# A decoder layer on one core: unit maxima turned as three bfloat16 parts, mask loads in two halves, penalty rows loaded earlier

## The chip, the cores and the metric

The kernel runs on one core of one Trainium2 chip. The metric is the device time of one execution in microseconds, a median over several runs. A profiled execution gives the trace; its own time is set beside its span, because every duration below comes from that one execution.

## What is computed

One post-norm decoder layer over x of 1024 tokens by 128 features, batch 1:

```
x = layernorm(x + self_attention(x))          # 16 heads of 8, one shared K and V head, no mask
x = layernorm(x + cross_attention(x, ctx))    # 16 heads of 8, ctx has 6404 keys
x = layernorm(x + ffn(x))                     # 8 experts, top-1, weighted by the router's maximum
scores = where(mask == 0, -1e9, Q @ K.T / sqrt(8)); softmax; @ V     # mask: int32, 1024 x 6404
```

The mask is 1024 rows of 6404 int32. In these inputs all its rows are alike, but the kernel reads all of it to find out: it counts in each column how many rows are live. The outputs are float32 and the scores need nearly float32 exactness, so queries and keys go to TensorE as a high and a low part.

## The kernel before, in words

**Units and steps.** A unit is two heads. There are 16 self units and 16 cross units (eight pairs of heads, twice, for the two halves of the tokens). The work of a unit is a row pass and a column pass. The row pass (`self_row`, L1518; cross: `row_products`, L1732) makes scores with tokens on partitions in a bank `RT`, and VectorE reduces each bank to maxima (L935; cross L952 and L953). The column pass (`self_col`, L1530; cross `col_product`, L1739) makes the same scores with keys on partitions in a bank `ST`, ScalarE takes exponentials (L1302), and TensorE multiplies them with the values into `O` (`add_values`, L1503). A self unit has 8 steps, a cross unit 10. The program is one list of steps `s`; step `s` does the column pass of step s, the row pass of step s + 16 and the values of step s - 1. So the row pass runs two self units ahead.

**The maxima.** The column pass needs the maximum subtracted. It enters as extra rows of the stacked operand: each head of a unit has 64 partitions of `Qs` (`STACK`), 32 of them hold the products of high and low parts (from partitions 1 and 67), and partitions 0, 33, 66 and 99 (`MAXROWS`) hold minus the maximum as a high and a low part for each of the two heads, against ones in K. Partitions 34 and 65 of K hold a penalty for masked keys (`PENROWS`).

The chain of one unit's maximum: VectorE folds the maxima (`finx`, L929); GpSimd splits them (`split_max`: a cast to float32r, L564, and a subtraction, L566); TensorE turns them against the identity (`turn_max`, L1481) into 16 partitions of `O`; ScalarE copies them to `mxr` (`max_copy`, L1238); SP loads them to the four rows of `Qs` (`max_rows`, issued at L315); TensorE waits for that load at the unit's first column (`have_max`). In the self units the turn stands 5 steps before that column (step 8g - 5), in the cross units 3 steps (`TURN`).

**The mask.** GpSimd issues 16 mask loads (`load_mask`, L541), each 128 rows by 3328 int32, into two buffers. Load m is issued when pass m - 2 is over and, from the fourth on, when the load of a named unit's max rows has landed (`max_in`). After each lands, GpSimd takes min(mask, 1) as bytes (L611) and adds them to a running sum (L617). The splits of the maxima of units 0 to 10 stand at fixed places between these passes (`MAX_AHEAD`, `MAX_BETWEEN`), all in GpSimd's one order; that of unit 11 follows the last pass, and behind it stands the first layernorm's work (L551 to L555), which TensorE needs at step 86.

**The queues.** GpSimd's loads go through one queue (q0, software), SP's through another (q1, hardware). Both use the core's 16 DMA engines.

**The penalty rows and the chunk.** At h = 13 of its list SP stores five pieces of the penalty to a DRAM row `pd`. At h = 14, after the max rows of unit 14, `more_keys` waits for the last chunk's keys and issues their four stores (L396). Behind these SP waits for the `pd` stores and loads `pd` to rows 34 and 65 of `Kr` and `Kc`. TensorE waits for those two loads (`pen_in`) before the first cross row, at step 112. GpSimd loads the chunk's keys only when the four stores have landed (`kd_more`).

Of the kernel before, what the change touches and what calls it, by code (L numbers as in the profile page):

```python
# [16 lines left out]
P = 128  # L17
# [21 lines left out]
MAXROWS = slice(0, 100, 33)  # L39
PENROWS = (34, 65)  # L40
# [5 lines left out]
LEAD = 16  # L46
SLOTS = 5
# [88 lines left out]
def decoder_layer(nc, t, out):  # L136
    ctx = ExitStack()
    with ctx:
# [51 lines left out]
        mxh = sb("mxh", [P, 2, 2, 4], F32R)  # L190
        mxr = sb("mxr", [16, 2, P])
# [39 lines left out]
        def experts_room(first):  # L231
# [31 lines left out]
            "rt_ready rt_free st_ready st_free pv mx mx_part mx_split mx_turned mx_copied max_in0 max_in1 "  # L263
# [49 lines left out]
        def _(sp):  # L313
# [24 lines left out]
            def max_rows(G):  # L338

                sp.wait_ge(S("mx_copied"), G + 1)  # L340
                load(Qs[MAXROWS, G % UNITS, :].bitcast(F32).rearrange("o (t f) -> o t f", f=P), mxr[:, G % 2, :],
                     f"max_in{G % 2}")
# [32 lines left out]
            def gather_x_queries(ph, parts=range(4)):  # L375

                if 0 not in parts:
                    for k in parts:
                        load(*q_part("x", k // 2, k % 2, 8 * ph, 8 * ph + 8), "xq_in")
                    return  # L380
                sp.wait_ge(S("pv"), 64 * (ph + 1))
                sp.wait_ge(S("xq_out"), 32 * (ph + 1))
                if ph:
                    sp.wait_ge(S("xq_in"), 80 * ph)
                load(Qs[MAXROWS, 8 * ph:8 * ph + 8, :].bitcast(F32).rearrange("o h q -> o (h q)"), zerof[:, :], "xq_in")
                for k in parts:
                    load(*q_part("x", k // 2, k % 2, 8 * ph, 8 * ph + 8), "xq_in")
# [22 lines left out]
            for h in range(UNITS):  # L410
# [88 lines left out]
        def _(pool):  # L499
# [22 lines left out]
            g_.memset(Qs[:, DIRECT:8, :].bitcast(F32), 0.0).then_inc(S("q_clean"), 1)  # L522

# [8 lines left out]
            def load_mask(m):  # L532
                q, w = m // 2, m % 2
                if m >= 2:
                    h = (m - 2) * 3 // 4
                    pool.wait_ge(S("mask_used"), m - 1)
                    if h:
                        pool.wait_ge(S(f"max_in{h % 2}"), 16 * (h // 2 + 1))
# [64 lines left out]
            for m in range(2 * QT):  # L603
# [4 lines left out]
                pool.wait_ge(S(f"mask_in{m % 2}"), 16 * (m // 2 + 1))  # L608
# [237 lines left out]
        def _(dve):  # L846
# [29 lines left out]
            for f in range(2):  # L876
# [4 lines left out]
                mark(v.tensor_tensor(rowc[:, f, 2:3], ident[:, 66 * f:66 * f + 1], ident[:, 66 * f + 33:66 * f + 34],  # L881
                                     ALU.add))
# [333 lines left out]
        def _(act):  # L1216
# [16 lines left out]
            def max_copy(G, bank=None):  # L1233
                act.wait_ge(S("mx_turned"), G + 1)
                if G >= 2:
                    act.wait_ge(S(f"max_in{G % 2}"), 16 * (G // 2))
                turned = O[0:16, 256:256 + P] if bank is None else ST[bank][0:16, 0:P]
                nc.scalar.copy(mxr[:, G % 2, :], turned).then_inc(S("mx_copied"), 1)  # L1238
# [178 lines left out]
        def _(pe):  # L1417
# [59 lines left out]
            def turn_max(G, bank=None):  # L1477
                pe.wait_ge(S("mx_split"), G + 1)
                rows = mxh[:, :, :, :].bitcast(F32).rearrange("p f k t -> p (f k t)")
                if bank is None:  # L1480
                    mm = mmul(O[0:16, 256:256 + P], rows, ident[:, :], start=False, stop=False, skip_group_check=True)  # L1481
                else:
                    mm = nc.tensor.transpose(ST[bank][0:16, 0:P], rows, ident[:, :])
                mm.then_inc(S("mx_turned"), 1)

            def have_max(G):
                pe.wait_ge(S(f"max_in{G % 2}"), 16 * (G // 2 + 1))
# [259 lines left out]
            def cross(gen):  # L1747
# [9 lines left out]
                def row(r, f):  # L1757
                    U, u = (r - SELF) // RU, (r - SELF) % RU
                    if f:
                        if u == 0 and U % 8 == 0:  # L1760
                            pe.wait_ge(S("xq_in"), 80 * (U // 8 + 1))
                            pe.wait_ge(S("pen_in"), 32)
# [193 lines left out]
```

## Time and profile before

| | us |
|---|---|
| median of 3 runs | 466.97 (466.77 to 467.68) |
| profiled execution, its own time | 469.97 |
| its span, first to last instruction | 467.7 |
| TensorE busy | 440.9 (94%) |
| VectorE busy | 396.7 (85%) |
| ScalarE busy | 358.4 (77%) |
| GpSimd busy | 245.1 (52%) |
| mean granted TensorE clock | 0.974 |

The page of the profile divides the span into 40 slices with each engine's busy share, the clock and the DMA rate. Behind it stand views of one line, one stretch or one tile, the chain of waits that ended last, and a timeline. TensorE's records are matmuls (PE) and weight loads (PEld). A float32 matmul is written as two records. An idle time in square brackets stands before the instruction and names who released it.

### The profile page before, as it was taken

To read this page: it belongs to the slowest core of one execution; us is meant where nothing else is said; L and a number is where in the kernel's file an instruction comes from. 1 tells how busy PE (TensorE), PEld (TensorE's weight loads), DVE (VectorE), ACT (ScalarE), POOL (GpSimd) and SP (SyncE) were. 2 spreads that over 40 slices of the span, in tenths; PEclk is the share of its full clock that TensorE was granted. 3 is DMA by queue.
4 is the path that set the end of the run, shared out by engine and by line. 5 is a ranking of instruction groups with operands and counts; after the bars stand their busy time and mean duration, and the time that the engine had idled before them with its cause. 6 is when DMAs were issued, how large, how long until landed. Compare 5 with 4: busy or idle time off the path is not lost.

```text
span 467.7 us, 10803 instructions
## 1 busy us (share of the span) xinstructions
PE 440.9 (94%) x3885; PEld 176.7 (38%) x3887; DVE 396.7 (85%) x522; ACT 358.4 (77%) x704; POOL 245.1 (52%) x381
## 2 busy tenths in 40 slices
PE   8999999999899999799999999999999999999983
PEld 2433333333334443233343334333443443333441
DVE  4989999999699689689998999999999999941455
ACT  6328889688677877588968988889868788878723
POOL 4726879976799604122447644444447254320453
PEclk9889999999899999989999999999999999999978
DMA  5849968679680073211232346322212122110000
GB/s 129 322 115 315 283 218 297 264 263 332 228 329 13 3 135 80 65 45 46 84 90 69 101 93 111 92 60 58 88 51 70 39 81 69 47 29 26 5 22 25
DMA packets 24595, 56.07 MB, mean 120 GB/s; under 512 B 6442, under 2 KB 15928, under 8 KB 22492
## 3 DMA queue, kind: packets, MB, share of 16 engines
q0 software_dynamic: 7536, 37.91, 24.6%
q1 hardware_dynamic: 16424, 17.24, 14.1%
q8 instruction: 33, 0.54, 0.5%
q10 hardware_dynamic: 580, 0.20, 0.2%
q14 instruction: 22, 0.18, 0.1%
HBM read 45.60 MB, written 9.18 MB: 117 GB/s over the span
## 4 chain that ended last, share of the span: by engine, by line
PE 76%; DVE 10%; DMA 5%; issue 4%; ACT 2%; POOL 2%; POOLq 0%; DVEq 0%; ACTq 0%
PE O L1503 29%; PE ST L1739 15%; PE ST L1530 9%; PE RT L1732 7%; DVE mxs L935 6%; DMA Qs<-mxr 5%; PE RT L1518 4%; PE RT L1625 2%; PE ST L1632 2%; PE RT L1429 1%; PE O L1481 1%; ACT prob L1302 1%; PE RT L1587 1%; PE RT L1595 1%; DVE mxc L952 1%
## 5 line engine op out<-in xcount | busy, mean ns | idle before, releaser
L1302 ACT ACTIVATE prob<-ST 128x512 f32<-128x512 f32 x512 | 279.5, 599 | 59.0 <-PE ST L1530 29.3
L935 DVE TENSOR_REDUCE mxs<-RT 128x2 f32<-128x1024 f32 x128 | 153.0, 1222 | 14.6 <-PE RT L1518 13.5
L952 DVE TENSOR_REDUCE mxc<-RT 128x2 f32<-128x1024 f32 x128 | 152.8, 1221 | 5.8 <-PE RT L1732 5.4
L1739 PE MATMUL ST<-Qs,Kc 64*128 64x512 f32 x320 | 117.4, 450 | 0.0
L1732 PE MATMUL RT<-Kr,Qs 64*128 64x512 f32 (+1 forms) x384 | 114.4, 400 | 2.1 <-issue 2.1
L1503 PE MATMUL O<-prob,vst 128*9 128x256 f32 x1280 | 99.1, 381 | 1.7 <-ACT prob L1291 0.5
L1530 PE MATMUL ST<-Qs,Kself 64*128 64x512 f32 x256 | 96.7, 449 | 4.0 <-DMA Qs<-mxr 3.8
L1518 PE MATMUL RT<-Kself,Qs 64*128 64x512 f32 x256 | 89.3, 465 | 2.2 <-DVE Kself L912 0.9
L681 POOL DMA_DIRECT2D Kr<-kd x96 | 47.8, 502 | 75.9 <-PE RT L1732 60.8
L1503 PE MATMUL O<-prob,Vs 128*9 128x256 f32 x1024 | 81.0, 388 | 1.2 <-ACT osb L1246 0.3
L1739 PEld LDWEIGHTS ST<-Qs,Kc 64*128 64x128 f32 x320 | 50.5, 184 | 65.8 <-issue 38.7
L1530 PEld LDWEIGHTS ST<-Qs,Kself 64*128 64x128 f32 x256 | 39.6, 186 | 55.9 <-ACT prob L1302 38.2
L1732 PEld LDWEIGHTS RT<-Kr,Qs 64*128 64x128 f32 x384 | 51.4, 185 | 2.8 <-issue 2.3
L611 POOL TENSOR_SCALAR big<-big 128x3328 uint8<-128x3328 uint32 x16 | 47.4, 2961 | 4.3 <-DMA big<-in_mask 3.9
L691 POOL DMA_DIRECT2D Kc<-kd x64 | 31.6, 497 | 33.9 <-PE ST L1739 31.6
L953 DVE TENSOR_REDUCE mxc<-RT 128x4 f32<-128x1024 f32 x32 | 38.9, 1223 | 4.8 <-PE RT L1732 4.6
L1503 PEld LDWEIGHTS O<-prob,vst 128*9 128x9 f32 x1280 | 19.4, 88 | 53.0 <-ACT prob L1302 16.2
L1518 PEld LDWEIGHTS RT<-Kself,Qs 64*128 64x128 f32 x256 | 35.3, 188 | 10.8 <-DVE mxs L935 5.0
L1291 ACT ACTIVATE prob<-ST 128x512 f32<-128x512 f32 x64 | 34.7, 595 | 5.2 <-PE ST L1739 3.6
L1503 PEld LDWEIGHTS O<-prob,Vs 128*9 128x9 f32 x1024 | 15.8, 88 | 48.1 <-ACT prob L1302 30.2
L617 POOL TENSOR_TENSOR big<-big 128x832 int32<-128x832 int32 x14 | 27.4, 1960 | 0.8
L564 POOL CAST mxh<-finx 128x8 fp32r<-128x8 f32 x32 | 6.1, 191 | 40.5 <-DVE finx L929 40.3
(219 smaller groups left out, 327.4 us busy)
## 6 DMA issues: line engine op xcount, KB each, us to landing
big<-in_mask POOLq DMA_DIRECT2D x16, 1664.0 KB, 7.3
Kc<-kd POOLq DMA_DIRECT2D x64, 80.0 KB, 2.2
Kr<-kd POOLq DMA_DIRECT2D x64, 64.0 KB, 2.1
od_s<-osb SPq DMA_DIRECT2D x16, 128.0 KB, 2.5
kd<-Vx SPq DMA_DIRECT2D x4, 512.0 KB, 6.9
Qs<-qd_x SPq DMA_DIRECT2D x8, 256.0 KB
od_x<-osb SPq DMA_DIRECT2D x14, 128.0 KB, 1.7
Qs<-qd_s SPq DMA_DIRECT2D x12, 128.0 KB, 5.9
```

Source lines behind the costliest of these rows:

```text
L611: g_.tensor_scalar(sums if q == 0 else dead8, maskI[m % 2].bitcast(U32), 1.0, 0.0, ALU.min, ALU.max) \
L681: pool.dma_start(Kr[r:r + PROD, w].bitcast(F32), head_rows(U, f)[:, w]).then_inc(S(f"kr{part}"), 16)
L935: freed(v.tensor_reduce(mxs[:, h % 2, c2, :].rearrange("p (f t) -> p f t", f=2)[:, :, q], bank[:, :].rearrange("p (f k) -> p f k", f=2), A ...
L952: return v.tensor_reduce(o[:, :, u % 4], src, AX.X, ALU.max)
L953: return v.tensor_reduce(o[:, :, 2 * (u - SRU):2 * (u - SRU) + 2], src.rearrange("p f (t k) -> p f t k", t=2), AX.X, ALU.max)
L1291: nc.scalar.activation(prob[:, s % SLOTS, f * HALF:(f + 1) * HALF], ST[ST_AT[s, f][2]][:, :], ACT.Exp) \
L1302: freed(nc.scalar.activation(prob[:, s % SLOTS, f * HALF:(f + 1) * HALF], bank[:, :], ACT.Exp))
L1503: mm = mmul(O[32 * q:32 * q + VW, 0:256], v[q // 2], prob[:, slot, q * 256:(q + 1) * 256], start=G is not None, stop=False, skip_group_che ...
L1518: mm = mmul(bank[:, f * HALF:(f + 1) * HALF], Qs[STACK[f], h, q * P:(q + 1) * P], Kself[STACK[f], c2 * 512:(c2 + 1) * 512], start=True, st ...
L1530: st_done(mmul(st_place((c, f))[:, :], Kself[STACK[f], b * P:(b + 1) * P], Qs[STACK[f], g, :], start=True, stop=True))
L1732: mm = mmul(o_, Qs[STACK[f], U, q * P:(q + 1) * P], Kr[STACK[f], w], start=True, stop=not gen, skip_group_check=True)
L1739: mm = mmul(o[:, :], Kc[STACK[f], b * P:(b + 1) * P], Qs[STACK[f], j, :], start=True, stop=not gen, skip_group_check=True)
```

## The change

Three edits. First, each maximum is split into three bfloat16 parts. `split_max` has four instructions in place of two, `turn_max` is one bfloat16 matmul of 24 columns of weights against a bfloat16 identity in place of a float32 one of 16, `max_copy` copies 24 partitions, and `max_rows` issues two DMAs: the four rows as before and a second one for rows 35 and 100 (`LASTROWS`). The K rows 35 and 100 are set to one. All waits on `max_in` count 32 in place of 16. The clearing of the max rows for the second half of the cross stage is two DMAs as well. Second, `load_mask` issues two DMAs of 64 partitions each (`MPART = 64`) on the same queue, and pass m waits for both. Third, the penalty loads stand at h = 13, right behind the `pd` stores, ahead of `more_keys`.

```diff
+LASTROWS = slice(35, 101, 65)
+MPART = 64
-        mxh = sb("mxh", [P, 2, 2, 4], F32R)
-        mxr = sb("mxr", [16, 2, P])
+        mxl = sb("mxl", [P, 1, 2, 4])
+        mxh = sb("mxh", [P, 6, 4], BF16)
+        identb = sb("identb", [P, P], BF16)
+        mxr = sb("mxr", [24, 2, P])
...
                 sp.wait_ge(S("mx_copied"), G + 1)
-                load(Qs[MAXROWS, G % UNITS, :]..., mxr[:, G % 2, :], f"max_in{G % 2}")
+                for rows, r0, r1 in ((MAXROWS, 0, 16), (LASTROWS, 16, 24)):
+                    load(Qs[rows, G % UNITS, :]..., mxr[r0:r1, G % 2, :], f"max_in{G % 2}")
...
-                load(Qs[MAXROWS, 8 * ph:8 * ph + 8, :]..., zerof[:, :], "xq_in")
+                for rows, r1 in ((MAXROWS, P), (LASTROWS, P // 2)):
+                    load(Qs[rows, 8 * ph:8 * ph + 8, :]..., zerof[0:r1, :], "xq_in")
...
                     for k, c in enumerate((*range(CHUNKS - 4, CHUNKS), CHUNKS - 5)):
                         load(pd[...], penr[...], "pen_out")
-                if h == 14:
-                    more_keys()
                     sp.wait_ge(S("pen_out"), 16 * 5)
                     sp.wait_ge(S("k_clean"), 2)
                     for k_ in (Kr, Kc):
                         load(k_[...], pd.to_broadcast([2, KUSE]), "pen_in")
+                if h == 14:
+                    more_keys()
...
-                pool.dma_start(maskI[m % 2], t["mask"][q * P:(q + 1) * P, w * HALFT:(w + 1) * HALFT]) \
-                    .then_inc(S(f"mask_in{m % 2}"), 16)
+                for p0 in range(0, P, MPART):
+                    pool.dma_start(maskI[m % 2][p0:p0 + MPART, :],
+                                   t["mask"][q * P + p0:q * P + p0 + MPART, w * HALFT:(w + 1) * HALFT]) \
+                        .then_inc(S(f"mask_in{m % 2}"), 16)
...
                 parts = finx[:, :].rearrange("p (f t) -> p f t", f=2)
-                g_.tensor_copy(mxh[:, :, 0, :], parts).then_inc(S("mx_part"), 1)
+                high = mxh[:, 0:4, :].rearrange("p (f k) t -> p f k t", k=2)
+                step(g_.tensor_copy(high[:, :, 0, :], parts))
+                step(g_.tensor_tensor(mxl[:, 0, :, :], parts, high[:, :, 0, :], ALU.subtract))
+                g_.tensor_copy(high[:, :, 1, :], mxl[:, 0, :, :]).then_inc(S("mx_part"), 1)
                 pool.wait_ge(S("mx_part"), G + 1)
-                g_.tensor_tensor(mxh[:, :, 1, :], parts, mxh[:, :, 0, :].bitcast(F32), ALU.subtract) \
+                g_.tensor_tensor(mxh[:, 4:6, :], mxl[:, 0, :, :], high[:, :, 1, :], ALU.subtract) \
                     .then_inc(S("mx_split"), 1)
...
-                rows = mxh[:, :, :, :].bitcast(F32).rearrange("p f k t -> p (f k t)")
-                    mm = mmul(O[0:16, 256:256 + P], rows, ident[:, :], ...)
+                o = O[0:24, 256:256 + P] if bank is None else ST[bank][0:24, 0:P]
+                mm = mmul(o, mxh[:, :, :].rearrange("p k t -> p (k t)"), identb[:, :], ...)
```

`step` adds a wait of GpSimd on its own instruction. The bfloat16 identity is one more cast on GpSimd at the start.

## Rows read from the trace of the kernel before

**Rows 1.** The page, busy time of each engine.

```profile
PE 440.9 (94%) x3885; PEld 176.7 (38%) x3887; DVE 396.7 (85%) x522; ACT 358.4 (77%) x704; POOL 245.1 (52%) x381
```

**Rows 2.** Stretches (start:end length, busy of PE, PEld, DVE, ACT, POOL, clock, DMA share, GB/s).

```profile
34.00:140.00 106.00, 100.19 (x940) 36.47 (x938) 97.28 (x93) 85.61 (x171) 84.64 (x66) 0.98 0.81 279
37.00:40.00 3.00, 3.00 (x32) 0.99 (x34) 3.00 (x4) 2.61 (x6) 1.61 (x2) 1.00 0.99 417
...
170.00:175.00 5.00, 4.72 (x46) 1.75 (x38) 4.87 (x9) 4.13 (x9) 0.39 (x2) 1.00 0.98 136
...
196.00:206.00 10.00, 8.30 (x65) 2.79 (x65) 6.07 (x6) 5.81 (x13) 3.56 (x9) 0.83 0.16 50
```

**Rows 3.** The page, DMA issues: count, KB each, us to landing.

```profile
big<-in_mask POOLq DMA_DIRECT2D x16, 1664.0 KB, 7.3
...
Qs<-qd_x SPq DMA_DIRECT2D x8, 256.0 KB
```

**Rows 4.** The chain that ended last, in three stretches: start us, us, what.

```profile
46.19 0.20 PE O L1481 x2
...
110.56 8.32 DMA Qs<-mxr
...
125.02 1.80 DMA Qs<-mxr
```

**Rows 5.** The waits: engine, line <- releaser: us in total, times, longest.

```profile
PE ST L1530 <- DMA Qs<-mxr: 3.8, 3, 2.6
```

**Rows 6.** GpSimd's timeline at the end of the mask passes.

```profile
127.38 0.60 POOL L541 DMA_DIRECT2D big<-in_mask  x1 [2.00 <-DMA Qs<-mxr]
...
145.96 0.20 POOL L566 TENSOR_TENSOR mxh<-finx,mxh 128x8 fp32r<-128x8 f32 x1
...
147.73 3.12 POOL L555 TENSOR_SCALAR x<-x,mv,rstd 128x128 f32<-128x128 f32 x4
```

**Rows 7.** TensorE's timeline at its turns and transposes there.

```profile
135.65 0.39 PE L1481 MATMUL O<-ident,mxh 128*16 128x128 f32 x2 [0.76 <-POOL mxh L566]
...
148.43 0.38 PE L1481 MATMUL O<-ident,mxh 128*16 128x128 f32 x2
...
152.38 0.66 PE L1602 MATMUL ST<-ident,x 128*128 128x128 f32 x4
```

**Rows 8.** Line 1429, bfloat16 matmuls of 512 columns: ns, first and last start.

```profile
L1429 PE MATMUL ST<-wrow x11: 379/379/380, 441.5 to 443.6; 128*128 128x512 bf16 x11
```

**Rows 9.** Timelines of one cross unit's maximum and the next unit's first column.

```profile
282.27 0.20 POOL L566 TENSOR_TENSOR mxh<-finx,mxh 128x8 fp32r<-128x8 f32 x1
...
283.00 0.38 PE L1481 MATMUL O<-ident,mxh 128*16 128x128 f32 x2
...
283.70 0.66 SPq L315 DMA_DIRECT2D Qs<-mxr  x1
...
286.96 0.50 PE L1739 MATMUL ST<-Qs,Kc 64*128 64x512 f32 x1
```

**Rows 10.** SP's timeline around the penalty.

```profile
179.89 1.44 SPq L315 DMA_DIRECT2D pd<-big  x5
...
191.72 2.92 SPq L396 DMA_DIRECT2D kd<-big  x4
...
195.71 0.60 SPq L315 DMA_DIRECT2D Kc<-pd  x1
```

**Rows 11.** The chain that ended last, at the first cross row.

```profile
193.46 0.55 PE O L1503 x8
...
194.67 0.55 PE O L1503 x8
...
195.64 2.06 issue
...
198.64 0.97 PE O L1503 x8
...
202.30 0.55 PE O L1503 x8
```

More of the change, by code:

```diff
@@ L262, in decoder_layer @@
             "ctx_in kd_out kd_more k_clean vx_ones kr0 kr1 kr2 kc0 kc1 vs0 vs1 mx_folded x_bias bias_tile dve_chain "
-            "rt_ready rt_free st_ready st_free pv mx mx_part mx_split mx_turned mx_copied max_in0 max_in1 "
+            "rt_ready rt_free st_ready st_free pv mx mx_part mx_split mx_turned identb_made mx_copied max_in0 max_in1 "
             "o_copied o_in0 o_in1 o_back o_last den_in rden var std xn xq_high xq_low xq_out xq_in "
@@ L340, in max_rows @@
                 sp.wait_ge(S("mx_copied"), G + 1)
-                load(Qs[MAXROWS, G % UNITS, :].bitcast(F32).rearrange("o (t f) -> o t f", f=P), mxr[:, G % 2, :],
-                     f"max_in{G % 2}")
+                for rows, r0, r1 in ((MAXROWS, 0, 16), (LASTROWS, 16, 24)):
+                    load(Qs[rows, G % UNITS, :].bitcast(F32).rearrange("o (t f) -> o t f", f=P), mxr[r0:r1, G % 2, :],
+                         f"max_in{G % 2}")
             def o_rows(G):
@@ L383, in gather_x_queries @@
                 if ph:
-                    sp.wait_ge(S("xq_in"), 80 * ph)
-                load(Qs[MAXROWS, 8 * ph:8 * ph + 8, :].bitcast(F32).rearrange("o h q -> o (h q)"), zerof[:, :], "xq_in")
+                    sp.wait_ge(S("xq_in"), 96 * ph)
+                for rows, r1 in ((MAXROWS, P), (LASTROWS, P // 2)):
+                    load(Qs[rows, 8 * ph:8 * ph + 8, :].bitcast(F32).rearrange("o h q -> o (h q)"), zerof[0:r1, :],
+                         "xq_in")
                 for k in parts:
@@ L522, in _ @@
             g_.memset(Qs[:, DIRECT:8, :].bitcast(F32), 0.0).then_inc(S("q_clean"), 1)
+            pool.wait_ge(S("cst"), 1)
+            g_.tensor_copy(identb[:, :], ident[:, :]).then_inc(S("identb_made"), 1)
             steps = [3]
@@ L537, in load_mask @@
                     if h:
[L538 removed]
+                        pool.wait_ge(S(f"max_in{h % 2}"), 32 * (h // 2 + 1))
                     else:
                         pool.wait_ge(S("q_in"), 16 * 4)
[L541 to L542 removed]
+                for p0 in range(0, P, MPART):
+                    pool.dma_start(maskI[m % 2][p0:p0 + MPART, :],
+                                   t["mask"][q * P + p0:q * P + p0 + MPART, w * HALFT:(w + 1) * HALFT]) \
+                        .then_inc(S(f"mask_in{m % 2}"), 16)
             def stack(o, hi, z, sign, name):
@@ L607, in _ @@
                 sums = acc8[:, w * HALFT:(w + 1) * HALFT]
-                pool.wait_ge(S(f"mask_in{m % 2}"), 16 * (m // 2 + 1))
+                pool.wait_ge(S(f"mask_in{m % 2}"), 16 * P // MPART * (m // 2 + 1))
                 if m >= 3:
@@ L880, in _ @@
                 mark(v.tensor_reduce(rowc[:, f, 1:2], ident[:, r + 2 * DH:r + PROD], AX.X, ALU.add))
-                mark(v.tensor_tensor(rowc[:, f, 2:3], ident[:, 66 * f:66 * f + 1], ident[:, 66 * f + 33:66 * f + 34],
-                                     ALU.add))
+                last = LASTROWS.start + 65 * f
+                mark(v.scalar_tensor_tensor(out=rowc[:, f, 2:3], in0=ident[:, 66 * f:66 * f + 1],
+                                            scalar=ident[:, 66 * f + 33:66 * f + 34], in1=ident[:, last:last + 1],
+                                            op0=ALU.add, op1=ALU.add))
                 mark(v.tensor_reduce(rowc[:, f, 3:4], parts[:, :, 0, :], AX.XY, ALU.add))
@@ L1235, in max_copy @@
                 if G >= 2:
-                    act.wait_ge(S(f"max_in{G % 2}"), 16 * (G // 2))
-                turned = O[0:16, 256:256 + P] if bank is None else ST[bank][0:16, 0:P]
+                    act.wait_ge(S(f"max_in{G % 2}"), 32 * (G // 2))
+                turned = O[0:24, 256:256 + P] if bank is None else ST[bank][0:24, 0:P]
                 nc.scalar.copy(mxr[:, G % 2, :], turned).then_inc(S("mx_copied"), 1)
@@ L1478, in turn_max @@
                 pe.wait_ge(S("mx_split"), G + 1)
-                rows = mxh[:, :, :, :].bitcast(F32).rearrange("p f k t -> p (f k t)")
[L1480 to L1483, printed above, removed]
+                if G == 0:
+                    pe.wait_ge(S("identb_made"), 1)
+                o = O[0:24, 256:256 + P] if bank is None else ST[bank][0:24, 0:P]
+                mm = mmul(o, mxh[:, :, :].rearrange("p k t -> p (k t)"), identb[:, :], start=bank is not None, stop=bank is not None,
+                          skip_group_check=True)
                 mm.then_inc(S("mx_turned"), 1)
             def have_max(G):
-                pe.wait_ge(S(f"max_in{G % 2}"), 16 * (G // 2 + 1))
+                pe.wait_ge(S(f"max_in{G % 2}"), 32 * (G // 2 + 1))
             def have_queries(h):
@@ L1760, in row @@
                         if u == 0 and U % 8 == 0:
-                            pe.wait_ge(S("xq_in"), 80 * (U // 8 + 1))
+                            pe.wait_ge(S("xq_in"), 96 * (U // 8 + 1))
                             pe.wait_ge(S("pen_in"), 32)
```

## The prediction

> **What bounds the kernel now.** I read the page first: TensorE is busy 94% of the span and VectorE 85% [rows 1], so TensorE bounds it wherever nothing stops it. Next the stretches. From 34 to 140 us, the self stage, GpSimd is busy 84.6 of 106 us and the 16 DMA engines 81% of the time at 279 GB/s, beside a full TensorE [rows 2]: three resources stand close together there and only there. The DMA issues say what fills the queue: 16 mask loads of 1664 KB, 7.3 us each from issue to landing [rows 3]. The chain of waits shows whom they hold up: the load of the max rows, 8 KB, took 8.32 us when issued right behind a mask load, and 1.80 us when nothing stood ahead of it [rows 4]. TensorE waited for such loads at three unit starts of the self stage, 3.8 us in all and 2.6 at the longest [rows 5]. The last stop is at the first cross row: 2.06 us and a slow stretch behind it [rows 11], in which the granted clock is 0.83 [rows 2]. The rest of the cross stage runs without waits.
>
> **The penalty loads.** They were issued behind the four stores of the chunk's keys: stores from 191.72, the second penalty load from 195.71, TensorE released at 197.70 [rows 10, 11]. Moved, they follow the `pd` stores of 179.89 to 181.33; with 1.8 us to land, as the small load of rows 4, 1.4 us for two issues and another 1.8 us they are in by 187, seven steps before the need at 195.6. SP is asked for nothing else until the max rows of unit 14, so the added wait on the `pd` stores holds up nobody, and the four stores, released by VectorE at 191.72, move neither way. Price: a step is 1.21 us (193.46 to 194.67), and the three steps from 194.67 to 202.30 took 7.63 us in place of 3.63. That is 4.0 us, 2.06 of waiting and 1.9 of low clock (a values group 0.97 against 0.55 us). The next thing that could be late is the chunk's keys, needed 8 steps after the first cross row; their stores are not moved. I take -4.0, bounds -2.0 and -4.0.
>
> **The turn.** Two float32 records cost the chain 0.20 us [rows 4]. A bfloat16 matmul of 512 columns comes every 0.21 us (2.1 us over ten intervals) [rows 8], so 128 columns are 0.053. Saved: 0.147 us a turn, if TensorE is what is waited for. VectorE, the next busiest, is at 97.3 of 106 us in the self stage beside TensorE's 100.2 [rows 2], so it lets this through. In the 11 turns up to the end of the mask passes the queue decides in my forecast and they give nothing; the 20 behind give 2.9 us.
>
> **The split.** Two instructions more on GpSimd. One takes 0.20 us [rows 9], and with a gap of 0.08 for the wait on itself two more are 0.55 us. In a cross unit the old pair ends at 282.47 (282.27 + 0.20) and the turn starts at 283.00 [rows 9]: 0.53 us of cover, gone to nothing. I charge 0.1 us for the wait that is left, in 11 cross units that have this distance: +1.1, bounds 0 and 0.2 each. Behind the split on GpSimd stand the copy of values and the loads for the next unit, 3 steps ahead of need.
>
> **The second max-row DMA.** SP needs 0.66 us for one [rows 9], so the last part lands at 283.70 + 0.70 + 1.80 = 286.2, plus 0.1 for the later turn; the unit starts at 286.96. Covered, 0.65 us left; without cover it would be 0.7 us a unit. The wider copy on ScalarE (24 partitions for 16) and the set-up work I cost at nothing: same columns, and the set-up stands in front of the first unit, where I take its cost as nothing, with 0.3 us (a cast) as the other end. The second zeroing DMA (half of a 64 KB one) stands ahead of loads that land long before use.
>
> **The mask loads.** This decides the time. GpSimd issues two where it issued one, +0.6 us each. More important is what a load of 64 rows does in the queue. The trace has no such load. It has one of all 128 rows, 417 GB/s at a DMA share of 0.99, and loads to 16 partitions (the `Qs<-qd_x` of rows 3), 136 GB/s at a share of 0.98 [rows 2]. So the engines were full both times and moved a third as much: what limits is where the data goes. An upper bound for half the rows is 417 GB/s, a lower one 136. If each halving costs the same factor, (136/417) to the power 1/3 = 0.69, it is 287. If half the rows give half the rate, it is 208. I take 230, nearer to the second, because both halves stand in one queue, every engine has its part of the first before its part of the second, and they are only a little out of step.
>
> The Trainium skill speaks against this edit outright (page SBUF — State Buffer, section "Can I just issue two DMAs to hit both halves?"): partitions 0 to 63 reach only half of the ports, and two DMAs to the two halves gained 6% over one. Its table (section Door 1) has 196 GB/s for 64 partitions at 1 MiB against 328 for all, and 104 for the first 16; for the last the trace has 136, so it agrees in kind. By 196 GB/s the sum below would give about 508 us, an estimate from that page.
>
> *Sum of the stage.* A mask load is 1.704 MB, so 4.09 us now; the 14 loads from the third on are 57.2 us of the 85.9 us (0.81 of 106) that the engines are busy; other traffic is 28.7 and 20.1 us are free. At 230 GB/s a load is 7.41 us, 14 are 103.7, with the rest 132.4: 26.4 us more than the stage has. It cannot run with no free time at all, because load m waits for a landing of max rows, which itself stands behind the loads ahead; I leave 4 us free (a fifth of what is free now), +30.4. GpSimd then ends its last pass that much later. The split of unit 11 ends at 146.16 [rows 6], its turn is at 148.43; the layernorm ends at 150.85, its transpose is at 152.38 [rows 7]. The smaller cover, 1.5 us, comes off: +28.9. All of TensorE's later work moves with it. What the stage's own waits cost now is in the free time already.
>
> Together: +28.9 - 4.0 - 2.9 + 1.1 = +23.1 us. The span goes from 467.7 to 490.8, the execution's own 469.97 to 493; counted on the median of 466.97, **490 us**.
>
> **Rivals.** (a) *The halves overlap.* Engines that finish their share of the first half fill the second while others are still in the first, and both together keep the old rate. From about 5.5 us a load (4.09 + 20.1/14, 310 GB/s) the queue is not the bound. Then: -4.0; turns -0.147 x 28 = -4.1; on GpSimd two more issues of 0.6 and a split of 0.55 between 127.38 and the turn at 135.65, which had no cover [rows 6, 7], +1.7; cross splits +1.1; the second max-row DMA at three unit starts that end on it, +0.7 each. Sum -3.2, **463.8 us**. For it: two transfers in one queue never fully keep step. Against it: the mask load of rows 2 has the engines in step at 0.99. This is the rival on the other side.
> (b) *The max rows slip in between the halves.* As (a), and the waits of rows 5 with their slow clock go, about 5 us, and the 2.1 too: **457 us**. Against it: the 8.32 us of rows 4 are longer than a whole mask load, so what stands ahead in the queue is served first, and both halves are issued within 1.2 us.
> (c) *The milder rate,* 287 GB/s: a load is 5.94 us, the sum of busy time 111.8 us, +5.8, with 4 us of free time and GpSimd's 1.7 it is about +9.5 - 5.8: **471 us**.
> (d) *Halves fully in step,* 208 GB/s: 8.17 us, 143.1 us, +37.1 + 4 - 1.5 - 5.8: **501 us**. It is the rule of the Trainium skill named above, as this kernel would meet it.
> (e) *The penalty loads don't help,* because the row waits for something else then: my forecast plus 4, 494 us; inside the range.
>
> **How the numbers follow.** Forecast with (e), 478 to 499 us: 0.47. (d) and above: 0.12. (c), 466 to 478: 0.14. (a), 460 to 466: 0.20. (b): 0.07. Both signs hold much, so the likeliest case's own range is 478 to 499. The range for 8 in 10 leaves out (b), the top of (d) and the edge of (a): 461 to 502. A difference under 0.2% (0.9 us) can't be told from none. Faster: (a), (b) and the edge of (c), 0.30; same 0.03; slower 0.67.
>
> **What would show it.** Right: a stretch inside a mask load with a DMA share near 1 and 200 to 250 GB/s; issue to landing of a half well above 5 us; GpSimd waiting for `in_mask` before most passes; the last pass ending near 175 us; TensorE waiting for the max rows or the split at most self unit starts, with low clock there; one turn record per unit; no stop before the first cross row. Wrong: over 310 GB/s inside a mask load. Then (a) or (b) holds, and the split and the second DMA are what is left of the price. The step most likely to fail is the rate of 230 GB/s.

## The result, and the profile after

| | ratio to before (95%) | median, us |
|---|---|---|
| predicted | 1.049 | 490 (461 to 502) |
| the changed kernel | 1.102 (1.094 to 1.111) | 515.87 (511.03 to 518.14) |
| before, the runs beside it | 1 | 467.33 (466.77 to 468.0) |

The direction was right. The size was not: 48.5 us were lost where 23.1 were forecast, and the time lies above the range. On the chips of the experiments the kernel before itself took from 464.8 to 472.7 us, so kernels are compared by their ratio to the runs of before on the same chip; a ratio leaves out the runs that are over 1.5% above the fastest of their kernel, and a median here counts them. A difference between two ratios is taken as shown only where their intervals are apart.

First the page of the changed kernel: busy time, the slices of the clock and of the DMA engines, the software queue, and the mask loads' issues (KB of one, median us from issue to landing).

```profile
PE 449.5 (87%) x3856; PEld 177.1 (34%) x3856; DVE 396.0 (77%) x522; ACT 358.5 (69%) x704; POOL 266.1 (52%) x462
PEclk9888859887997968999999999999999989999988
DMA  5967994997898880072312223453231212211001
q0 software_dynamic: 7792, 37.91, 32.2%
big<-in_mask POOLq DMA_DIRECT2D x32, 832.0 KB, 10.4
```

TensorE's share fell from 94 to 87% [rows 1] and what it lost is in the left half of the slices, where the clock is low too. The queue moved the same 37.91 MB and took 32.2% of 16 engines' span for it, where it was 24.6%. A half of a mask load lands 10.4 us after its issue; the whole one took 7.3 [rows 3].

The stretches of the changed kernel answer to [rows 2]. Columns: window, length, busy time of PE, PEld, DVE, ACT and POOL, granted clock, DMA share, GB/s. In the first only mask loads run.

```profile
13.00:20.00 7.00, 6.82 (x34) 3.75 (x32) 7.00 (x7) 3.30 (x6) 6.83 (x6) 1.00 1.00 213
34.00:140.00 106.00, 77.81 (x643) 27.16 (x643) 67.00 (x61) 60.79 (x119) 61.76 (x65) 0.82 0.85 184
34.00:200.00 166.00, 122.64 (x1020) 44.32 (x1020) 107.43 (x109) 95.16 (x187) 101.04 (x103) 0.84 0.83 184
41.00:194.40 153.40, 113.32 (x956) 40.73 (x955) 99.25 (x94) 88.68 (x175) 95.73 (x98) 0.84 0.87 193
```

A load of 64 rows runs at 213 GB/s with the engines full, half of the 417 of [rows 2]. That is the forecast's 230 less 7%. But the engines are not full over the stage: from the issue of the third mask load at 41.0 us to the landing of the last at 194.4 the share is 0.87, so about 20 of 153 us are free, where the forecast left 4. The next two views of the changed kernel say who waits: TensorE's and GpSimd's waits (us in total, times, longest).

```profile
PE ST L1546 <- DMA Qs<-mxr: 38.6, 6, 10.5
PE O L1498 <- POOL mxh L580: 8.3, 4, 5.7
```

```profile
POOL mxh L576 <- DVE finx L945: 40.1, 21, 11.0
POOL big L625 <- DMA big<-in_mask: 21.9, 8, 5.7
POOL big L551 <- DMA Qs<-mxr: 20.2, 5, 5.3
```

Against 3.8 us in [rows 5], TensorE now waits 38.6 us for max rows, and 8.3 us for the split where the kernel before has this row:

```profile
PE O L1481 <- POOL mxh L566: 0.8, 1, 0.8
```

So these two waits went from 4.6 to 46.9 us. TensorE's busy time grew by 8.6 us, from 440.9 to 449.5; the two together, less the 2.1 us of the stop that is gone, are the 48.8 us by which the span is longer (516.5 against 467.7). GpSimd waits in two directions: 21.9 us for masks, and 20.2 us for max rows before it may issue masks. The chain shows two units of it (start us, us, what):

```profile
41.80 0.63 SPq L319
42.47 9.39 DMA Qs<-mxr
51.90 1.22 PE ST L1546 x2
53.12 0.97 PE O L1519 x8
54.09 1.15 PE ST L1546 x2
55.24 0.55 PE O L1519 x8
...
57.49 0.69 SPq L319
58.23 15.30 DMA Qs<-mxr
73.58 0.79 PE ST L1546
```

The max rows of a unit (an 8 KB load and a 4 KB one) are in 9.4 and 15.3 us after the second of them was issued, behind mask halves in the other queue; the worst of before was 8.32 [rows 4]. Behind each stop the clock is low for some steps: from 52 to 54 us the granted clock is 0.50, and a values group takes 0.97 us at 53.12 and 0.55 at 55.24. The granted clock over 34 to 140 us is 0.82, where it was 0.98.

### The profile page after: what moved, and what is told of

It reads as the page before. It is cut to its first block, busy times and chain, and to the rows that moved or that the text cites. A ratio compares the mean times of both kernels' runs of the same rounds, so it can differ in the third digit from the quotient of the medians.

```text
span 516.5 us, 10858 instructions
## 1 busy us (share of the span) xinstructions
PE 449.5 (87%) x3856; PEld 177.1 (34%) x3856; DVE 396.0 (77%) x522; ACT 358.5 (69%) x704; POOL 266.1 (52%) x462
## 3 DMA queue, kind: packets, MB, share of 16 engines
q0 software_dynamic: 7792, 37.91, 32.2%
## 4 chain that ended last, share of the span: by engine, by line
PE 62%; DMA 18%; DVE 6%; POOL 5%; issue 4%; ACT 3%; SPq 2%; POOLq 0%; DVEq 0%; ACTq 0%
PE O L1519 23%; PE ST L1755 13%; DMA Qs<-mxr 12%; PE ST L1546 7%; PE RT L1748 6%; DMA big<-in_mask 3%; PE RT L1534 2%; DMA qd_s<-Vx 2%; DVE mxs L951 2%; PE RT L1641 2%; SPq L319 1%; PE ST L1648 1%; POOL big L625 1%; PE RT L1445 1%; ACT prob L1318 1%
## 5 line engine op out<-in xcount | busy, mean ns | idle before, releaser
L1546 PE MATMUL ST<-Qs,Kself 64*128 64x512 f32 x256 | 105.2, 489 | 38.7 <-DMA Qs<-mxr 38.6
L1534 PE MATMUL RT<-Kself,Qs 64*128 64x512 f32 x256 | 99.1, 500 | 2.3 <-DVE Kself L928 0.9
L1519 PE MATMUL O<-prob,Vs 128*9 128x256 f32 x1024 | 85.5, 408 | 1.0 <-ACT osb L1262 0.3
L1546 PEld LDWEIGHTS ST<-Qs,Kself 64*128 64x128 f32 x256 | 43.5, 206 | 95.8 <-ACT prob L1318 43.8
L625 POOL TENSOR_SCALAR big<-big 128x3328 uint8<-128x3328 uint32 x16 | 47.4, 2965 | 22.0 <-DMA big<-in_mask 21.9
L1534 PEld LDWEIGHTS RT<-Kself,Qs 64*128 64x128 f32 x256 | 39.7, 206 | 9.2 <-DVE mxs L951 4.9
L969 DVE TENSOR_REDUCE mxc<-RT 128x4 f32<-128x1024 f32 x32 | 38.9, 1224 | 4.8 <-PE RT L1748 4.6
L551 POOL DMA_DIRECT2D big<-in_mask x32 | 17.7, 556 | 32.6 <-DMA Qs<-mxr 20.2
## 6 DMA issues: line engine op xcount, KB each, us to landing
big<-in_mask POOLq DMA_DIRECT2D x32, 832.0 KB, 10.4
```

The lines of the kernel that those rows point to most:

```text
L625: g_.tensor_scalar(sums if q == 0 else dead8, maskI[m % 2].bitcast(U32), 1.0, 0.0, ALU.min, ALU.max) \
L969: return v.tensor_reduce(o[:, :, 2 * (u - SRU):2 * (u - SRU) + 2], src.rearrange("p f (t k) -> p f t k", t=2), AX.X, ALU.max)
L1519: mm = mmul(O[32 * q:32 * q + VW, 0:256], v[q // 2], prob[:, slot, q * 256:(q + 1) * 256], start=G is not None, stop=False, skip_group_che ...
L1534: mm = mmul(bank[:, f * HALF:(f + 1) * HALF], Qs[STACK[f], h, q * P:(q + 1) * P], Kself[STACK[f], c2 * 512:(c2 + 1) * 512], start=True, st ...
L1546: st_done(mmul(st_place((c, f))[:, :], Kself[STACK[f], b * P:(b + 1) * P], Qs[STACK[f], g, :], start=True, stop=True))
```

## The experiments

**1 to 4. Which part costs, and what of the halves.** The first undoes the halves, the second does the halves alone, the third and the fourth halve the load in other ways.

```diff
e1_whole_masks, from the changed kernel:
-MPART = 64
+MPART = 128
e2_halves_alone: the kernel before with load_mask of the changed one
e3_every_second_row, from the changed kernel, in load_mask:
+for p0 in range(2):
+    pool.dma_start(maskI[m % 2][p0:P:2, :], t["mask"][q * P + p0:(q + 1) * P:2, ...])
e4_column_halves:
+for c0 in range(0, HALFT, HALFT // 2):
+    pool.dma_start(maskI[m % 2][:, c0:c0 + HALFT // 2], ...)
```

> The changed kernel with each mask load whole again, one DMA of 128 rows; the three-part turn, the third row with its second DMA, and the moved penalty loads stay. Theory A (the halves cost the whole loss, because 64 adjacent partitions take a transfer at half the rate): a mask load is back at about 410 GB/s, its issue-to-landing at 7.3 us, and the time is that of the rest of the change by the prediction's own terms, 462 to 465 us (466.97 - 4.0 for the penalty loads, -4 to 0 for the turns, +1 to +3 for splits and second max-row DMAs). Theory B (the later max rows, three-part split and second DMA, make the mask loads' gate late and cost a good part by themselves): 475 us or more, with TensorE waiting for the max rows at more than three unit starts of the self stage.

> The kernel before with one edit: each mask load as two DMAs of 64 rows. Theory A: inside a mask load 213 GB/s, and the time is that of the changed kernel plus what the rest of the change gives, 517 to 523 us. Theory B (the second max-row DMA behind each half doubles the delay, so that the parts make each other worse): 495 us or less, since there is one max-row DMA per unit here.

> The changed kernel with the two DMAs taking the even and the odd rows of the tile (64 partitions each, spread over all 128) in place of the lower and the upper 64. Bytes, number of DMAs and rows per DMA are as in the changed kernel. Theory A1 (where the 64 partitions lie sets the rate: adjacent ones share half of the ways into SBUF): about 400 GB/s inside a load, a packet of 13312 B back near 0.5 us, time as with whole masks, 462 to 467 us. Theory A2 (any DMA of 64 rows, or any pair of DMAs, runs at half rate whatever its partitions are): 213 GB/s and 512 to 519 us.

> The changed kernel with each mask load as two DMAs of all 128 rows and half the columns (6656 B of a row each). Theory A1: full rate, 400 GB/s or more, and the time of whole masks within 2 us, 462 to 467 us, +0.6 us of GpSimd's time for each load included. Theory A2 (two DMAs for one are the cost): 500 us or more. Rival (b) of the prediction, max rows slipping in between two halves: 457 us or less, the longest wait of TensorE for max rows in the self stage under 2 us where it was 2.6.

Measured, with the stretch from 13 to 20 us read in each:

| | ratio (95%) | median, us | GB/s, 13 to 20 us |
|---|---|---|---|
| e1, whole | 1.001 (0.998 to 1.005) | 469.62 | 404 |
| e2, lower and upper 64 rows, alone | 1.087 (1.081 to 1.092) | 509.96 | 219 |
| e3, even and odd rows | 0.999 (0.994 to 1.003) | 471.71 | 411 |
| e4, halves of the columns | 1.000 (0.997 to 1.004) | 469.45 | 411 |

The rows of e3 and of e2 for that stretch:

```profile
13.00:20.00 7.00, 6.82 (x34) 3.89 (x34) 7.00 (x7) 3.00 (x5) 6.83 (x6) 1.00 0.99 411
```

```profile
13.00:20.00 7.00, 6.82 (x34) 3.93 (x32) 7.00 (x7) 2.53 (x4) 6.83 (x6) 0.93 1.02 219
```

The DMA share is the same, about 1; the bytes are not. So the loss is in the halves (theory A), and it is neither in having two DMAs nor in 64 rows: it is in which 64 partitions. Halving by even and odd rows, or by columns, costs nothing that can be told by the ratios; the ten runs of e3 spread from 465.2 to 477.0 us, and by the medians it would be 0.6% slower than before, so a cost of that size isn't excluded for even and odd rows. Two things missed: e2 came out at 510 us instead of 517 or more, so the rest of the change, which was to give something back, adds 1.5% beside slow masks; and e1, e3 and e4 did not reach the 462 to 465 or 467 us expected.

**5 to 8. What the rest does beside slow masks.**

```diff
e6_halves_second_dma, from e2: a second max-row DMA, waits on max_in count 32,
and a second clearing DMA before each half of the cross stage
-load(Qs[MAXROWS, G % UNITS, :]..., mxr[:, G % 2, :], f"max_in{G % 2}")
+for rows, r0, r1 in ((MAXROWS, 0, 16), (LASTROWS, 0, 8)):
+    load(Qs[rows, G % UNITS, :]..., mxr[r0:r1, G % 2, :], f"max_in{G % 2}")
e7_halves_and_pen, from e2: the penalty loads ahead of more_keys()
e8_no_gate, from the changed kernel, in load_mask:
-    if h:
-        pool.wait_ge(S(f"max_in{h % 2}"), 32 * (h // 2 + 1))
-    else:
+    if not h:
```

> The changed kernel once more, as the measure for the three beside it: 512 to 519 us.

> The kernel before with the mask loads in halves of 64 rows and, as the one further part, a second max-row DMA per unit (its content, a copy of the first eight rows, goes to rows 35 and 100, which the kernel before does not use; the turn stays float32 in two parts). Halves alone came to 510 us, the changed kernel to 516. Theory S (the second DMA stands behind what the queues hold and ends each unit's landing later, which in a stage gated both ways costs every unit): 514 to 518 us, with TensorE waiting over 32 us for the max rows in the self stage (halves alone: 27.6). Theory G (the longer split on GpSimd is what the halves do not bear): 508 to 512 us, waits as with halves alone.

> The kernel before with the mask loads in halves and the penalty loads moved. The term of the prediction: -4.0 us against halves alone, 504 to 508 us, with the 2.1 us stop at the first cross row gone. Theory N (the stop goes but something else holds the row, as the chunk's keys with the clock low anyway): 509 to 511 us.

> The changed kernel whose mask loads no longer wait for a unit's max rows (the buffer's own wait, and the first one's for the queries, stay). Theory L (the stage is gated both ways: a mask load waits for a landing that stands behind mask loads, so the engines stand idle 17% of 34 to 200 us): the DMA share of that stretch goes to 0.92 or more, the last pass comes 10 to 20 us earlier and the time is 498 to 508 us. Theory P (the gate protects: without it two whole loads, 16 us at this rate, stand ahead of each unit's max rows, and TensorE loses more than the masks gain): 516 to 530 us, with TensorE's waits for the max rows over 45 us.

The changed kernel again took 514.8 us median, but one of its four runs was 504.95 and the others 513.0 to 516.8, so it has no ratio of its own here. The second DMA on top of the halves gave 1.105 (1.096 to 1.114), 517.8 us: 1.8% or 8.6 us, give or take 5, for a 4 KB DMA a unit. That is theory S; TensorE's waits, e6 (27.6 us in e2 for the first row):

```profile
PE ST L1537 <- DMA Qs<-mxr: 35.4, 8, 11.1
PE O L1488 <- POOL mxh L573: 6.2, 2, 4.9
```

With the penalty loads moved, the halves came to 1.080 (1.069 to 1.092), 506.4 us: 2.9 us less by the ratios and 3.5 by the medians, inside the bounds of the prediction, though the intervals overlap. Without the gate (e8) nothing was won: 517.7 us, 1.100 (1.090 to 1.110). TensorE waited 44.0 us for max rows; GpSimd no longer waits the 20.2 us of the gate, but its waits for folded maxima went from 40.1 to 61.5 us:

```profile
PE ST L1544 <- DMA Qs<-mxr: 44.0, 10, 10.3
```

```profile
POOL mxh L574 <- DVE finx L943: 61.5, 23, 11.5
```

Theory L is out. Theory P had the time (516 to 530 us) and nearly the wait (over 45 us), but its claim that the gate protects isn't shown either: with and without it the ratio is the same within its interval. So the loss isn't made by the gate.

The landings tell more than the waits. From the issue of a unit's first max-row DMA to the last landing of its rows, summed over units 0 to 12 in the trace of each:

| | sum, us | ratio |
|---|---|---|
| before | 50.2 | 1 |
| penalty loads alone (e9) | 50.5 | 0.991 |
| all but the halves (e1, e11) | 56.3, 57.0 | 1.001, 1.003 |
| halves alone (e2), with the penalty loads (e7) | 84.1, 84.4 | 1.087, 1.080 |
| halves and second DMA (e6) | 96.6 | 1.105 |
| the changed kernel | 97.2 | 1.102 |
| without gate (e8) | 103.0 | 1.100 |

Halves alone add 34 us to the landings and 40.5 us to the time, the second DMA 12.5 and 8.6. The two need not go together: with column halves (e4) the landings are 50.9 us, some 6 less than in e1 and e11, and the time is that of e1.

Where in the program the time goes shows in single traces by the issue of unit 12's max rows, behind the last mask pass. It comes at 162.65 us before, 203.73 in e2, 211.06 in e6 and 216.03 in the changed kernel: +41.1 for the halves, +7.3 for the second DMA and +5.0 for the rest, all of it ahead of the cross stage. The third mask load, with which the stage begins, is issued at 34.4 us before, at 38.9 in e2 and at 41.0 in the changed kernel, because the first two loads hold up the stores of the queries: the queries' first loads, which wait for these stores, are issued at 22.7 us before and at 30.5 in the changed kernel.

**9 to 12. The two other parts with whole loads.** The parts of the change alone: e9 the penalty loads, e10 the three-part turn with its split and second DMA, e11 both (the kernel of e1), and e12 the penalty loads with masks in column halves, as in e4.

```diff
e9_pen_alone, from the kernel before:
-                if h == 14:
-                    more_keys()
                     sp.wait_ge(S("pen_out"), 16 * 5)
                     ... (the two loads to Kr and Kc)
+                if h == 14:
+                    more_keys()
e10_turn_alone: the changed kernel, MPART = 128, and this edit undone
e12_columns_and_pen: e9 with load_mask of e4
```

> The kernel before with the penalty loads moved and nothing else. The term of the prediction is -4.0 us (bounds -2.0 and -4.0): a ratio of 0.991 to 0.996, the stop at the first cross row gone and its slow stretch with it. Theory N (the clock would be low there anyway, the stop costs only itself): -2 us, ratio 0.996.

> The kernel before with the three-part bfloat16 turn, its split and its second max-row DMA; masks whole, penalty loads where they were. By the terms of rival (a) it should come to about +0.8 us: -4.1 for the turns, +1.7 and +1.1 for splits, +2.1 for the second DMA. Theory T (what the second DMA and the split cost in the self stage is two to three times that, since every landing is 0.6 us later or more and eleven units wait for one): +3 to +6 us, a ratio of 1.006 to 1.013, TensorE waiting over 7 us for max rows and split together in the self stage, where it was 4.6 before.

> The changed kernel with whole mask loads once more, beside its two parts on one chip: the sum of the two ratios' distances from 1, within 0.3%, so 0.998 to 1.005.

> The kernel before with the penalty loads moved and each mask load as two DMAs of all 128 rows and half the columns. If the halves let max rows in between them (rival (b)'s mechanism), landings of max rows in the self stage sum to under 45 us where they were 50.2 for 13 units, and the time is 1 to 3 us below the penalty loads alone. If what stands ahead is served first whatever its form, it is that time, plus up to 1 us for GpSimd's 14 further issues.

| | ratio (95%) | median, us |
|---|---|---|
| e9, penalty loads | 0.991 (0.987 to 0.995) | 462.55 |
| e10, turn | 1.008 (1.004 to 1.011) | 472.28 |
| e11, both | 1.003 (1.000 to 1.006) | 470.05 |
| e12, penalty loads, column halves | 0.993 (0.989 to 0.996) | 464.48 |

The penalty loads are worth 4.1 us (2.2 to 5.9), as predicted. The chain of e9 at its first cross row answers to [rows 11]: no stop, and the values group at 0.55 us from the first on.

```profile
197.18 0.39 PE O L1481 x2
197.57 0.42 PE ST L1530
198.00 0.24 PE RT L1732 x2
...
198.24 0.55 PE O L1503 x8
```

The stop, 2.1 to 2.2 us, is in the traces of before, e2, e6 and e10, which leave the penalty loads where they were; the low clock behind it isn't in all of them. It stands in the traces of before and e6 (values groups of 0.97 us), and not in those of e2 and e10. The rows of e2:

```profile
236.76 2.10 issue
...
239.56 0.55 PE O L1506 x8
```

From unit 12's max rows to unit 16's, the loads moved save 3.3 us against before (53.2 to 49.9), 2.1 us in e7 against e2 and 1.6 in e11 against e10. So about 2 us are sure, and the other 2 come with the low clock. Single spans tell no more than that: the stretch behind unit 31's max rows, which no edit touches, takes 47.7 us in e1, 49.4 in e11, the same kernel, and 51.1 in before, at granted clocks of 0.95, 0.92 and 0.90.

The turn costs 3.6 us where rival (a)'s terms made it 0.8, and TensorE waits 8.7 us for max rows and split in the self stage (e10): theory T. The parts add up to -0.1% and measure +0.3%, a little further apart than the 0.3% expected, with intervals as wide as that. Where e11 loses against e9 its waits say; first e9's, then e11's:

```profile
PE ST L1530 <- DMA Qs<-mxr: 2.1, 1, 2.1
...
PE O L1481 <- POOL mxh L566: 1.4, 3, 0.7
```

```profile
PE O L1498 <- POOL mxh L580: 5.3, 4, 2.9
PE ST L1546 <- DMA Qs<-mxr: 4.5, 4, 2.0
```

6.3 us more waiting, 5.6 of it before unit 12 (4.1 in e1, the same kernel as e11): unit 12's max rows are issued at 164.40 in place of 160.50. Behind it the turn does give something: from there to unit 31's, e9 takes 250.8 us and e11 249.6, since an undisturbed cross unit is 12.51 us long where it was 12.62. Rival (b) found no support in e12: landings 49.3 us, where under 45 were its sign, and a ratio that can't be told from e9's.

**13 to 18. What was still open.** Four questions: whether the second DMA is late by its later issue (e14 with halves, e15 with whole loads, ScalarE issues it right behind its copy); whether GpSimd's order was the rest of the gate (e16); how the rate goes with adjacent rows (e13, e17); whether halves in two queues overlap (e18).

```diff
e13_quarters: MPART = 32;  e17_sixteen_rows: MPART = 16
e14_second_on_act, e15_whole_second_on_act (MPART = 128), in max_copy:
+    act.wait_ge(S("mx_copied"), G + 1)
+    act.dma_start(Qs[LASTROWS, G % UNITS, :]..., mxr[16:24, G % 2, :])
e16_load_first, from e8, in the loop over m: load_mask(m + 2) right behind the pass
e18_two_queues, on SyncE ahead of the first queries:
+for m in range(2):
+    load(maskI[m][MPART:P, :], t["mask"][MPART:P, m * HALFT:(m + 1) * HALFT], f"mask_up{m}")
```

> The changed kernel with each mask load as four DMAs of 32 adjacent rows. It is run for the rate: 417 GB/s was read for 128 rows, 213 for 64, 136 for 16. Theory W (the rate follows the share of the ways into SBUF that the rows reach, with a floor): 32 rows give 107 to 140 GB/s, and the time is over 600 us. Theory F (each halving costs the same factor, the curve through 417 and 136 that the prediction drew with 0.69 for each): 195 GB/s or more for 32 rows, and 213 for 64 was the odd one.

> The changed kernel with the second max-row DMA issued by ScalarE right behind its copy, in place of SyncE 0.7 us behind the first. Theory S1 (the second landing is late because it is issued later, and a mask load slips ahead of it in some units): landings come within 1 us of each other and 4 to 8 us of the 8 that the second DMA cost come back, 506 to 512 us. Theory S2 (a second DMA of any kind is late behind the masks, it meets the same engines): within 2 us of the changed kernel, 513 to 518 us.

> As the run above with whole mask loads: the candidate that keeps the three-part turn. With it on SyncE the kernel came to a ratio of 1.003, the penalty loads alone to 0.991. Theory S1: 0.990 to 0.997, cross units 12.5 us long where they were 12.6. Theory S2: 1.001 to 1.005.

> The changed kernel in which a mask load waits neither for a unit's max rows nor for the split of a unit's maxima: it is issued right behind the pass that frees its buffer. With the semaphore alone taken away the time stayed at 517.7 us, DMA share 0.87 from 34 to 140 us. Theory Q (GpSimd's order was the other half of the gate; a late unit then holds back the split, and the split the next load): the share goes to 0.95 or more and the last pass ends 10 to 25 us earlier, the time at 495 to 510 us. Theory P (a queue filled earlier only puts more ahead of the max rows, and TensorE loses what the masks gain): 515 us or more, TensorE waiting over 45 us for the max rows.

> The changed kernel with each mask load as eight DMAs of 16 adjacent rows. 128 rows gave 417 GB/s, 64 and 32 both 213. Theory W (what counts is which ways into SBUF the rows reach; 16 adjacent rows reach half of what 32 and 64 reach): 105 to 136 GB/s inside a mask load, a packet of 13312 B at 1.6 to 2.0 us, and over 570 us. Theory H (the only limit is that the rows lie in one half of the partitions): 213 GB/s, 505 to 518 us.

> The changed kernel in which the upper halves of the first two mask loads are issued by SyncE, in its own queue, at the same time as GpSimd issues the lower ones; the 14 other loads as in the changed kernel. Read is the stretch from 13 to 20 us, in which only these loads run. Theory O (halves in two queues run beside each other and reach all ways into SBUF together, so that it is their sharing one queue, in step, that halves the rate): 350 GB/s or more there, packets of both halves at once, the first passes and the query stores earlier, 505 to 512 us. Theory I (a transfer of 64 adjacent rows halves the engines' rate whatever runs beside it): 213 GB/s there and the time of the changed kernel.

*The rate.* The stretch from 13 to 20 us with parts of 32 rows (e13), of 16 rows (e17), and with the halves in two queues (e18):

```profile
13.00:20.00 7.00, 6.48 (x33) 3.74 (x32) 6.79 (x7) 2.88 (x5) 6.80 (x7) 1.00 1.00 213
```

```profile
13.00:20.00 7.00, 3.26 (x13) 1.45 (x12) 4.13 (x4) 3.00 (x5) 6.88 (x12) 1.00 1.02 129
```

```profile
13.00:20.00 7.00, 6.82 (x35) 3.92 (x36) 7.00 (x7) 2.69 (x5) 6.83 (x6) 1.00 0.98 223
```

32 adjacent rows run as fast as 64. Theory W of e13 is out by its rate, and theory F by its curve: its 195 GB/s or more was met, but it has 64 rows 1.45 times as fast as 32, and they are equal. 16 rows run at 129 GB/s, a packet of 13312 B at 1.64 us where it was 0.50 in 128 rows and 1.0 in 64, as theory W of e17 had it. The kernel in quarters took 508.35 us (one run, inside the spread of the changed kernel's eight, 504.95 to 518.14), the one in sixteen rows 595.93 (one run). The Trainium skill states this very pattern (page SBUF — State Buffer, section Door 1): rows 0 to 31 and 0 to 63 reach the same eight of 16 ports, because the bit that stands for 32 in a row's number chooses none. The runs agree, 213 and 213 GB/s, and even rows, which by the same section's formula reach all 16, with 411. In e18 the two queues did not run beside each other to any use: 223 GB/s and 516.29 us (one run), theory I. By the packets' start times the two queues were served mostly in turn, for one to two us each.

*The second DMA.* On ScalarE it was issued in the same 0.01 us as the first, and still landed late: in unit 2 of e14 both are issued at 56.70 and the last lands at 73.68, 17.0 us later, where it was 16.0. The time was 1.110 (1.104 to 1.115), against the changed kernel's 1.102; with whole loads (e15) 1.023 (1.020 to 1.026), worse than on SyncE. Theory S1 is out; both times lie above S2's ranges too, by a cost of its own: the issue holds ScalarE for 0.64 us a unit and the cross units are 12.92 us long instead of 12.51.

*The order.* e16 took 516.05 us, 1.100 (1.095 to 1.104): theory P by the time, though the wait stays under its 45 us. DMA share from 34 to 140 us 0.88, where e8 had 0.87, TensorE's waits for max rows:

```profile
PE ST L1544 <- DMA Qs<-mxr: 41.5, 8, 11.4
```

The last mask load is issued at 167.1 us in place of 178.8, 12 us earlier, and nothing of it reaches the end. That what a mask gains by standing further ahead is lost by the max rows behind it fits this, and isn't shown apart. What keeps the engines free for the rest of that stretch I can't show. Splits still stand ahead of passes (`MAX_AHEAD`), and GpSimd waits 58.4 us for folded maxima there; whether that is it was not tried.

## Why the prediction was wrong, by its steps

- **Rate of a half, 230 GB/s. Failed,** as it was feared. Measured 213 to 219. With 213 a load is 8.0 us, 14 are 112.0, the stage's sum is 140.7 us, and by the prediction's own working (4 us left free, 1.5 of cover) the masks cost +37.2 instead of +28.9. That alone would have made the forecast 498 us, inside its range; the time left the range by the next two steps. The error was in the choice between bounds: the curve of equal factors from 417 to 136 doesn't exist, the rates are 417, 213, 213, 129. The argument for 230 over 208, that the halves are a little out of step, gave 5 to 11 GB/s. The rule of the Trainium skill that was quoted against the edit (page SBUF — State Buffer, section "Can I just issue two DMAs to hit both halves?"), that two DMAs to the two halves gain only 6% over one, is what the runs show, 223 GB/s from two queues against 213 from one. It was given 0.12.
- **The second max-row DMA, "covered". Failed.** It is covered in the cross stage, as the sum had it. In the self stage, where it was costed only in rival (a), it adds 8.6 us (give or take 5) beside halves (e6 over e2): a second transfer behind mask loads that take twice as long.
- **The first two mask loads, at nothing. Failed.** The sum begins with the third load and lets the stage start when it did. At half the rate the first two hold up the queries, and the third is issued 4.6 us later in e2 and 6.6 in the changed kernel. With this term and 213 GB/s the working gives +41.8 us for halves alone; they cost +40.5 (37.9 to 43.1), and the last pass of e2 ends 41.8 us later. So the model of the stage held.
- **In the stage up to the last pass the turn gives nothing. Wrong in sign.** The split and the DMA lengthen a loop that runs through the queue: max rows late, TensorE late, next maxima late. Beside whole loads this loop takes 6.3 us of waiting more (e11 over e9), beside halves the second DMA alone 8.6 us of time. The longer split was not run by itself.
- **Free time of the stage, 4 us. Nearly held for the halves alone:** the DMA share is 0.94 in e2 from the third load's issue to the last one's landing (39.0 to 182.5 us), 9 us free. It failed for the whole change, 20 us. From 34 to 140 us the share is 0.94 in e2 and 0.85 in the changed kernel; with the gate gone or the loads moved up it is 0.87 and 0.88, and the time is the same.
- **The turn, -2.9, and the cross splits, +1.1.** One bfloat16 record per unit as predicted (31 in `O`, of 226 ns each as recorded, for 62 of 273). A cross unit is 0.11 us shorter; over 19 units 1.2 us were gained by the profiles, with the price of the splits in it, where -1.7 was expected for that stretch. Right within 0.5 us.
- **The penalty loads, -4.0. Right in size:** -4.1 (0.9913, 0.987 to 0.995), and the 2.06 us stop [rows 11] is in the waits of no kernel that has them moved. Half of the term is the low clock behind the stop, which only two of the four traces with the stop show; the 4.0 was read from one that does, so that it came out so near is in part luck. Rival (e) is out.
- **Rivals.** (a) 463.8 for halves that overlap: in one queue they don't, in two they don't either (e18). Its list of prices can be held against e11 and e1, the same kernel: -3.2 predicted, +1.5 and +0.6 us measured. Waits for the split and for max rows were to grow by 3.8 us and grew by 5.2 in e11 (9.8 against 4.6 before); turns and cross splits were to give 3.0 and gave 1.2 by the profiles. (b) Columns did not let max rows in (e12). (c)'s +9.5 is +10.0 by its own terms (5.8 + 4 + 1.7 - 1.5), 471 us either way. (d), fully in step, had the rate right (208) and came to 501 because it had no late start and took 5.8 us off for the rest, which costs some 7 us instead.

By the ratios, -2.9 (penalty loads beside halves), +40.5 (halves, the late start in them) and +8.6 (second DMA) are 46.2 of the 47.9 us. The 1.7 us left, for the split and the turn, are well inside the intervals, and no run separates them.

The best version is the penalty loads alone: 462.55 us, 0.9% below before. Column halves add nothing to it.

## What to carry to other kernels

A DMA engine's busy share says nothing of its rate: at a share of 1.0 the same bytes went at 417, 213 and 129 GB/s, by which partitions the transfer touched. To cut a load in two, cut the columns or take every second row, and never the lower and the upper half. And where a small transfer that shares the DMA engines with large ones releases the bottleneck, price a further transfer by what stands ahead of the small one at each step of the loop. The queue's free time priced the slower loads here to about 1 us, once rate and start were right, and it did not see the second DMA. Two edits can share one cover: apart, the halves (+40.5), the turn (+3.6) and the penalty loads (-4.1) make 40 us, and together they cost 47.9.

## What the runs showed that was not expected

- 32 adjacent rows load at the rate of 64 (213 GB/s both), and 64 rows taken evenly over 128 at the full one (411).
- Halves in two queues moved 223 GB/s together, hardly more than in one.
- A 4 KB DMA that adds 0.6 us to a landing when nothing stands ahead (2.38 us in e11's unit 11, 1.78 in e9's) adds 8.6 us (give or take 5) to the kernel beside slow loads.
- The stop at the first cross row brings the low clock with it in two traces of four.
- A DMA issue on ScalarE lengthened each undisturbed cross unit by 0.41 us, though ScalarE was busy only 77% of the span before.
